# A decoder layer on one core: the written lists of steps of all engines laid out anew

## The reference

```python
def attn(x):                      # RWKV time mixing
    xs = shift x by one token
    k = (x * tm_k + xs * (1 - tm_k)) @ Wk.T      # v and r in the same way
    r = sigmoid(r)
    wkv = recurrence over tokens of k, v         # _wkv, a scan in time
    return (r * layernorm(wkv)) @ Wo.T
def xattn(x, ctx):                # the same kind of recurrence, k = norm(x), v = ctx
def ffn(x):                       # (silu(x @ G.T * gs) * (x @ U.T * us)) @ D.T * ds, inner width 1408
x = x + attn(layernorm(x)); x = x + xattn(layernorm(x), ctx); x = x + ffn(layernorm(x))
```

## Time and profile before

| what | value |
|---|---|
| median of 3 runs | 600.77 us (599.24 to 601.04) |
| the profiled execution | 598.28 us |
| its span in the trace | 596.4 us |
| PE busy | 536.3 us, 90% |
| DVE busy | 457.1 us, 77% |
| ACT busy | 345.4 us, 58% |
| POOL busy | 53.4 us, 9% |

### The profile page before, as it was taken

How to read it: one execution, slowest core, us unless ns; L and a number is a source line. 1 busy time by engine, 2 the same in 40 slices (tenths; PEclk the granted TensorE clock), 3 DMA queues, 4 the chain that set the end, 5 groups by cost and what they waited for, 6 DMA issues and landing times.

```text
span 596.4 us, 8018 instructions
## 1 busy us (share of the span) xinstructions
PE 536.3 (90%) x2658; PEld 381.6 (64%) x2658; DVE 457.1 (77%) x742; ACT 345.4 (58%) x546; POOL 53.4 (9%) x155
## 2 busy tenths in 40 slices
PE   2998589677799999999889999999969999999995
PEld 2443444323398446885689446786768699989994
DVE  5999778996977489999857589999856499852433
ACT  4737783467868257676557447766644486634221
POOL 2000300101022003000103003000011100000000
PEclk9999699988989999999979999999979999999998
DMA  8999700012100000001060000001040010010001
GB/s 304 414 315 385 291 0 2 18 35 87 48 26 2 1 1 0 1 19 53 1 213 0 0 0 1 0 18 53 0 142 0 1 38 36 0 36 1 2 36 38
DMA packets 14261, 39.02 MB, mean 65 GB/s; under 512 B 1232, under 2 KB 1232, under 8 KB 14032
## 3 DMA queue, kind: packets, MB, share of 16 engines
q1 hardware_dynamic: 14224, 38.57, 18.0%
HBM read 34.37 MB, written 12.85 MB: 79 GB/s over the span
## 4 chain that ended last, share of the span: by engine, by line
issue 38%; PE 34%; DVE 15%; POOL 6%; ACT 5%; DMA 1%; DVEq 0%; POOLq 0%; SPq 0%; ACTq 0%
PE gu L722 13%; PE dacc L650 7%; PE bank L636 6%; PE bank L698 5%; PE bank L625 3%; POOL t_rstd L598 2%; DVE t_slot L954 2%; DVE t_st L1091 1%; ACT L745 1%; DVE t_slot L1099 1%; DVE t_otile L1149 1%; DVE t_slot L1046 1%; POOL t_veps L596 1%; ACT t_z L799 1%; DVE t_xf L1116 1%
## 5 line engine op out<-in xcount | busy, mean ns | idle before, releaser
L722 PE MATMUL gu<-t_z4h,t_gate 128*128 128x256 f32 x352 | 94.1, 299 | 7.9 <-DVE t_z4l L1123 7.5
L722 PE MATMUL gu<-t_z4l,t_gate 128*128 128x256 f32 x352 | 89.3, 286 | 0.0
L722 PE MATMUL gu<-t_z4l,t_up 128*128 128x256 f32 x352 | 89.3, 286 | 0.0
L722 PE MATMUL gu<-t_z4h,t_up 128*128 128x256 f32 x352 | 89.2, 285 | 0.0
L879 ACT ACTIVATE t_h<-gu,t_fsc 128x256 f32<-128x256 f32 x88 | 40.4, 472 | 67.3 <-PE gu L722 65.8
L722 PEld LDWEIGHTS gu<-t_z4h,t_gate 128*128 128x128 f32 x352 | 68.4, 194 | 12.7 <-issue 10.4
L650 PE MATMUL dacc<-t_down,t_hh 128*128 128x512 f32 x176 | 72.5, 412 | 1.8 <-DVE t_hl L973 1.8
L722 PEld LDWEIGHTS gu<-t_z4l,t_gate 128*128 128x128 f32 x352 | 68.3, 194 | 2.4 <-issue 1.7
L650 PE MATMUL dacc<-t_down,t_hl 128*128 128x512 f32 x176 | 69.0, 392 | 0.0
L1128 DVE SCALAR_TENSOR_TENSOR t_h<-gu,t_fsc,t_h 128x256 f32<-128x256 f32 x88 | 40.6, 476 | 36.0 <-ACT t_h L879 35.9
L722 PEld LDWEIGHTS gu<-t_z4h,t_up 128*128 128x128 f32 x352 | 68.1, 193 | 0.0
(11 more groups left out here) (129 smaller groups left out, 930.5 us busy)
## 6 DMA issues: line engine op xcount, KB each, us to landing
t_mixv<-in_x SPq DMA_DIRECT2D x8, 512.0 KB, 6.0
t_xres<-in_x SPq DMA_DIRECT2D x8, 512.0 KB, 5.5
t_ctxt<-in_ctx_t SPq DMA_DIRECT2D x16, 256.0 KB, 2.8
out<-t_otile SPq DMA_DIRECT2D x16, 256.0 KB, 2.2
gate_words<-in_gate_t SPq DMA_DIRECT2D x1, 2816.0 KB, 17.1
up_words<-in_up_t SPq DMA_DIRECT2D x1, 2816.0 KB, 24.3
t_gate<-gate_words SPq DMA_DIRECT2D x1, 2816.0 KB, 15.5
down_words<-in_down_t SPq DMA_DIRECT2D x1, 2816.0 KB, 23.1
```

The lines of the kernel that those rows point to most:

```text
L722: last = pe.matmul(gu[u % 2][:, side, :], as_read(w[:, k, i * P:(i + 1) * P], exact), as_read(part[:, k, hf * HALF:(hf + 1) * HALF], exact ...
```

## The change

Every list of steps is written in a new order. The set of steps of each engine is the same, and so are the instructions of each step; one wait is added (`tanh_done` ahead of each `rw` on DVE). On PE, in the start, the output projection `wo` of batch 0 stands right behind `turn1+`, ahead of all projections of batch 1, and `y` of batch 0 behind `v2+`. In a round, `k0` to `k3`, `v0`, `v1` of the next batch stand ahead of `wo`, and `r0`, `r1`, `r2` come ahead of `turn3`; in the last stages only neighbours are exchanged. On SP the large transfer `words2` stands ahead of the loads of batch 1, and in a round the loads of the next `x` come first.

```diff
     PE_FIRST = """
-        turn1 k0 k1 v0 v1 k2 k3 v2 v3 r0 r1 r2 r3 turn2 return2 turn1+ k0+ k1+ v0+ wo v1+ turn3 r0+ r1+
-        r2+ r3+ y k2+ k3+ v2+ v3+ turn4_0 flag
+        turn1 k0 k1 v0 v1 r0 k2 k3 v2 r1 r2 v3 r3 turn2 return2 turn1+ wo k0+ k1+ v0+ v1+ turn3 r0+ r1+
+        r2+ r3+ k2+ k3+ v2+ y v3+ flag turn4_0
         """.split()
     PE_BODY = """
-        up0 up1 turn4_1 up2 turn2 up3 up4 up5 return2 down0 up6 down1 turn1 up7 wo k0 k1 v0 k2 k3 down2
...
+        up0 turn4_1 up1 turn2 up2 up3 up4 return2 up5 down0 down1 up6 turn1 down2 down3 up7 k0 k1 v0 v1
+        k2 k3 up8 wo v2 v3 r0 r1 r2 up9 turn3 up10 down4 up11 down5 down6 up12 down7 up13 down8 down9
+        down10 up14 up15 r3 down11 down12 down13 up16 up17 up18 up19 down14 down15 up20 up21 down16 y
+        down17 down18 down19 down20 down21 turn4_0
         """.split()
     DVE_FIRST = """
...
-        mixr0+ mixr1+ mixr2+ mixr3+ nv0+ num0+ part0+ den1+ x1_0 x1_1 x1_2 x1_3 fin0+ norm4 nv1+ norm5
...
+        mixr3+ x1_0 x1_1 x1_2 x1_3 norm4 front0+ norm5 front1+ den0+ nv0+ num0+ part0+ nv1+ den1+ num1+
...
     SP_FIRST = """
-        words1 xload0+ xload1+ words2 ctx2 ctx3
+        words1 words2 xload0+ xload1+ ctx2 ctx3
         """.split()
     SP_BODY = """
-        ctx0 ctx1 rload0 rload1 xload0 xload1 ctx2 ctx3 out0 out1 out2 out3
+        xload0 xload1 ctx0 ctx1 rload0 rload1 out0 out1 ctx2 ctx3 out2 out3
         """.split()
...
                 elif kind(s) == "rw":
                     c = int(s[2:])
                     need(dve, lnt_done, b, c + 1)
+                    need(dve, tanh_done, b, c + 1)
```

More of the change, by code:

```diff
@@ L98, in decoder_layer @@
-        tanh1+ tanh2+ xfront3 xpart2 tanh3+ xpart3 weigh2 sq6 weigh3 front2+ front3+ weigh4 norm6 weigh5
-        part2+ z4_0_0 z4_0_1 part3+ flag
+        share_r1 share_r2 share_r3 front0 front1 part0 tanh0 part1 front2 front3 weigh0 part2 tanh1
+        tanh2 tanh3 part3 weigh1 weigh2 norm2 norm3 rw0 rw1 rw2 rw3 norm0+ norm1+ share_k0+ share_k1+
+        share_k2+ share_k3+ share_v0+ share_v1+ share_v2+ share_v3+ share_r0+ share_r1+ share_r2+
+        share_r3+ sq4 sq5 front0+ front1+ norm4 norm5 part0+ weigh3 part1+ xfront0 xfront1 weigh4 weigh5
@@ L100, in decoder_layer @@
+        xpart0 xpart1 xfront2 tanh0+ xfront3 tanh1+ xpart2 xpart3 tanh2+ tanh3+ front2+ front3+ sq6
+        norm6 part2+ z4_0_0 z4_0_1 part3+ flag
         """.split()
     ACT_BODY = """
[L103 to L106, removed]
@@ L107, in decoder_layer @@
-        silu15 high6 xfront0 high7 xfront1 silu16 silu17 xpart0 high8 xpart1 xfront2 xfront3 silu18
-        silu19 tanh0 tanh1 tanh2 tanh3 xpart2 high9 xpart3 silu20 silu21 high10 sq6 norm6 z4_0_0 z4_0_1
+        sq7 norm7 z4_1_0 z4_1_1 silu0 silu1 high0 silu2 norm2 norm3 silu3 high1 rw0 rw1 silu4 rw2 rw3
+        norm0 norm1 silu5 high2 share_k0 share_k1 share_k2 share_k3 share_v0 share_v1 share_v2 share_v3
+        silu6 silu7 high3 front0 front1 part0 share_r0 share_r1 share_r2 part1 front2 share_r3 silu8
@@ L130, in decoder_layer @@
[L130 to L133, removed]
+        stat1_0 stat1_1 norm0 norm1 mixk0 mixk1 mixk2 mixk3 mixv0 mixv1 mixv2 mixv3 mixr0 mixr1 front0
+        mixr2 mixr3 front1 nv0 nv1 den0 num0 part0 den1 num1 part1 fin0 front2 fin1 front3 nv2 den2 num2
@@ L134, in decoder_layer @@
+        front3+ nv2+ den2+ num2+ xf_0 xf_1 xf_2 xf_3 part2+ den3+ nv3+ flag norm6 num3+ part3+ fin2+
+        z4_0_0 z4_0_1 fin3+
         """.split()
     DVE_BODY = """
[L137 to L144, removed]
+        norm7 z4_1_0 z4_1_1 prod0 prod1 stat2_0 stat2_1 prod2 norm2 rest0 norm3 prod3 stat1_0 stat1_1
@@ new lines, in decoder_layer @@
+        rest1 prod4 norm0 norm1 prod5 rest2 mixk0 mixk1 mixk2 mixk3 mixv0 mixv1 mixv2 prod6 mixv3 rw0
+        rw1 rw2 rw3 prod7 front0 front1 den0 nv0 nv1 num0 part0 den1 num1 mixr0 mixr1 fin0 part1 front2
+        fin1 front3 x1_0 mixr2 x1_1 x1_2 rest3 mixr3 den2 x1_3 nv2 num2 nv3 part2 den3 num3 part3 fin2
+        norm4 fin3 prod8 norm5 prod9 xfront0 xfront1 xin0 xden0 xnum0 xpart0 prod10 xin1 prod11 rest4
+        xden1 xnum1 xpart1 prod12 rest5 prod13 xfin0 xfront2 rest6 out0 out1 prod14 xfin1 xfront3 xin2
@@ L145, in decoder_layer @@
+        xden2 xnum2 prod15 xin3 prod16 xpart2 prod17 xden3 rest7 xnum3 prod18 prod19 rest8 xpart3 xfin2
+        xfin3 rest9 prod20 prod21 xf_0 xf_1 rest10 out2 norm6 out3 xf_2 xf_3 z4_0_0 z4_0_1
         """.split()
     DVE_NEXT = """
-        norm7 prod0 z4_1_0 z4_1_1 prod1 prod2 stat2_0 stat2_1 prod3 rest0 norm2 norm3 rw0 rw1 rw2 rw3
-        prod4 x1_0 x1_1 prod5 norm4 x1_2 rest1 rest2 x1_3 norm5 prod6 prod7 xfront0 xfront1 xin0 xden0
-        xnum0 xin1 prod8 prod9 xpart0 xden1 xnum1 rest3 xpart1 prod10 prod11 xfin0 rest4 xfront2 rest5
@@ L151, in decoder_layer @@
-        xfin1 prod12 prod13 xfront3 out0 out1 xin2 prod14 prod15 xden2 rest6 xnum2 prod16 rest7 prod17
-        xpart2 xden3 prod18 xin3 xnum3 prod19 xpart3 xfin2 xfin3 rest8 xf_0 xf_1 rest9 prod20 prod21
+        norm7 z4_1_0 z4_1_1 prod0 prod1 stat2_0 stat2_1 prod2 norm2 norm3 prod3 rw0 rw1 rw2 rw3 x1_0
+        rest0 x1_1 prod4 prod5 rest1 x1_2 x1_3 norm4 norm5 prod6 xfront0 xfront1 xin0 xin1 xden0 prod7
+        rest2 xnum0 prod8 rest3 xpart0 prod9 xden1 xnum1 xpart1 prod10 prod11 rest4 xfin0 xfin1 xfront2
@@ L153, in decoder_layer @@
+        rest5 xfront3 prod12 prod13 xden2 xin2 rest6 xin3 prod14 out0 prod15 out1 xnum2 prod16 xpart2
+        prod17 xden3 xnum3 rest7 xpart3 prod18 prod19 xfin2 xfin3 rest8 xf_0 xf_1 rest9 prod20 prod21
         norm6 rest10 z4_0_0 z4_0_1 out2 out3 xf_2 xf_3
@@ L170, in decoder_layer @@
     POOL_NEXT = """
[L171 removed]
+        nb7 rn7 rn2 rn3 nb4 nb5 rn4 rn5 nb6 rn6
         """.split()
```

48 lines of the change are left out of this document (22 added, 26 removed).

## The result

The changed kernel takes 604.7 us (median of 10 runs, 602.48 to 651.22) against 600.39 of the kernel before in the same session (10 runs, 597.96 to 601.04): a ratio of 1.0072, with a 95% interval of 1.0059 to 1.0085. I had forecast 599.2. (The run of 651.22 had a mean granted clock of 0.82, against 0.94 to 0.95 in the others, and isn't in the ratio.) The profiled execution took 604.17 us, its span is 602.2, against 598.28 and 596.4.

A forecast was written before the change was run, and what follows sets the result against it. The prediction took VectorE to bound the start and PE the rounds. Its terms, +1.0 for the start, -1.0 for each of two rounds and -0.6 for the last stages, gave 600.8 - 1.6 = 599.2 us, range 595.4 to 603.2.

The forecast's parts named there:

- `words2` ahead of the loads: Start, SP: batch 1's loads land behind `t_down`, so its statistics start at 70.4, 2.6 us later.
- the rest of the start, `wo` first: Start: `wo` first delays `front0+` to 98.05 but leaves VectorE less work and fewer waits behind it; -1.6 us.
- rounds and last stages: Two rounds at -1.0 us each and the last stages at -0.6: -2.6 us together.
- The step that failed: VectorE: the added wait on `tanh_done` concerns work that ended some 10 us earlier, so it costs nothing.
- Its other half: Head of a round: `turn4_1` one `up` earlier costs nothing, as `xf_3` moves up 0.6 us; without cover 0.6.
- `wo` ahead of the projections: Start, PE: `wo` runs 79.65 to 94.6, losing 1.2 us to the low clock, bounds 0.4 and 2.1.
- my slower rival: Start: `front0+` is later still, as `turn1+` ends later or `wo` runs longer at low clock; 603.2 us, chance 0.22.
- my 1.0: Each round 1.0 us shorter, bounds -1.5 and +1.5.
- the waits of 0.70, 0.48 and 0.19: Rounds, PE: the waits ahead of `down10`, inside `y` and ahead of `down20` go, gross 1.4 us.
- the 0.4 that I kept back for `y`, `xin2` and `wo`: Rounds: 0.4 us of the gross 1.4 left for possible new waits of `y`, `xin2` and `wo`.
- the 2.06 and 2.49 stay: Rounds, PE: the waits of 2.06 us ahead of `turn4_0` and 2.49 ahead of `up0` remain.
- The last stages: Next stage: the 0.57 us wait ahead of `turn4_0` goes; last stage keeps PE full; -0.6 us, bounds -1.0 and 0.

The follow-up runs named there:

- padding: The change with eight one-column memsets added at the start of VectorE's list: 598.38 us, ratio 0.9962 to the kernel before.
- The mixture: Against the kernel before: new start lists but old order of the loads on SP, old rounds and last stages, eight memsets on VectorE: 600.68 us, ratio 0.9999.
- its partner's: The kernel before with eight one-column memsets at the start of VectorE's list and nothing else: 601.12 us, ratio 0.9997.
- the padded kernel with the old loads: The change with batch 1's loads again ahead of `words2` on SP in the start, and eight memsets on VectorE: 595.42 us, ratio 0.9906.
- the mixture with the old start: The change with all engines' start lists as before, new rounds and last stages, eight memsets on VectorE: 598.20 us, ratio 0.9951.
- before, four memsets: The kernel before with four one-column memsets added at the start of VectorE's list: 602.56 us, ratio 1.0025.
- the change, loads held back: The change, with SP holding each round's six loads until VectorE has written the last z4 of the batch before: 598.37 us, ratio 0.9959.
- the change without the first waits: The change without the added wait on `tanh_done` for the four `rw` of batch 0: 599.53 us, ratio 0.9997.

## Why the prediction was wrong, point by point

The ledger, each line a difference of medians (some pairs from two sessions, whose medians of the kernel before differ by 0.3 us at most). The lines are links of one chain of kernels, so that their sum comes near the whole by construction and is no check of its own:

| part | predicted | measured | between |
|---|---|---|---|
| `words2` ahead of the loads | +2.6 | +3.0 to +3.6 | three pairs |
| the rest of the start, `wo` first | -1.6 | -0.4 (within the scatter) | 600.68 and 601.12 |
| rounds and last stages | -2.6 | -5.3 and -5.6 | 595.42 and 600.68; 598.38 and 603.95 |
| the code's position: padding | 0 | +6.3 | 604.7 and 598.38 |
| of it, the four added waits alone | 0 | +5.2 | 604.7 and 599.53 |
| sum, with 6.3 for the position | -1.6 | +3.3 to +4.2 | the change: +4.3 |

**The step that failed: "The added wait on `tanh_done` concerns work that ended some 10 us earlier: nothing."** True of the wait and false of its instruction. Its four for batch 0 moved the loop by four instructions in VectorE's code, and the branch back to the head then needed a second fetch before `norm7`. Without them the change takes 599.53 us, nearly the 599.2 of the forecast, though by errors that cancel, as the ledger shows.

**Its other half: "`turn4_1` comes one `up` earlier ... I cost it at nothing; without that cover it would be 0.6."** I counted the cover against `xf_3` alone. A second fetch ahead of `norm7` costs the kernel before 2.0 us, with two `up`s in front of `turn4_1`, and the change 6.3 with one. The trace of the kernel before has a row of VectorE that idles 2.65 us at that place, which the prediction doesn't look at: the branch and the first fetch lie in it, and the loop's first instruction ran only 0.6 us ahead of `norm7`.

**The order of the loads** was right in kind and short in size. The first row of VectorE's statistics of batch 1 in the changed kernel, and SP's queue:

```profile
54.69 0.37 SPq L529 DMA_DIRECT2D t_down<-down_words  x1
55.10 5.06 SPq L494 DMA_DIRECT2D t_mixv<-in_x  x1
...
70.66 1.28 DVE L980 BATCH_NORM_STATS2 t_stats<-t_mixv 128x6 f32<-128x512 f32 x2 [3.33 <-DMA t_mixv<-in_x]
```

70.66 stands against 70.4 forecast and 67.83 before. The transfers land in the order of issue: `t_down` at 69.3, the halves at 70.6 and 71.9, where I had 69.0, 70.4 and 71.7. Loads that pass `t_down`, which the second half of the rule quoted from the Trainium skill ("DMA: Bandwidth & Descriptors", "Queues, rings and completion order") would have allowed, didn't show.

**`wo` ahead of the projections** is mis-sized by the clock. PE in the changed kernel, from the turn on:

```profile
77.25 1.97 PE L625 MATMUL bank<-t_ident,t_mixv 128*128 128x128 f32 x8 [0.89 <-DVE t_mixv L988]
79.94 16.13 PE L698 MATMUL bank<-t_wo,t_tanh_r 128*128 128x512 f32 x32 [0.72 <-ACT t_zt L810]
95.90 5.31 PE L636 MATMUL bank<-t_mixk,t_wk 128*128 128x512 f32 x12
...
79.94:96.07 16.13, 16.13 (x33) 7.11 (x34) 10.19 (x18) 9.58 (x18) 1.43 (x5) 0.87 0.00 0
```

`wo` took 16.13 us and not 13.75, at a mean granted clock of 0.87: 2.4 us lost, where I had bounds of 0.4 and 2.1 and took 1.2. The clock stayed at 1.2 GHz until 84.3, 4.3 us into `wo`. VectorE's scan behind `k0+` began at 99.54, 1.5 us later than forecast (98.05), and the first `up0`, forecast at 166.3, came at 167.71. VectorE's part was right: from `front0+` to the end of `z4_0_1` (167.56) it took 68 us, as summed. With the larger loss my -1.6 becomes -0.4. The mixture measured -0.4 too, but its runs and its partner's spread over 3 to 4 us, so the agreement to a tenth is luck. That VectorE's whole chain hangs on `k0+` was the mechanism of my slower rival; it made 1.5 us here, and the 101.5 from which that rival would decide was not reached.

**The rounds** gained more than the forecast. The first round became 1.5 us shorter against my 1.0: the waits of 0.70, 0.48 and 0.19 are gone in full, and the 0.4 that I kept back for `y`, `xin2` and `wo` wasn't needed. In the padded kernels a round is shorter by 2.1 to 2.9 us than with the old lists after the same start. Round two of the padded kernel with the old loads, and of its partner with the old lists:

```profile
301.69:435.99 134.30, 129.50 (x665) 94.27 (x665) 113.86 (x181) 87.76 (x139) 12.36 (x36) 0.98 0.09 32
```

```profile
302.43:439.33 136.90, 130.75 (x664) 94.42 (x665) 112.52 (x181) 83.59 (x135) 14.58 (x36) 0.97 0.09 31
```

Of the 2.6 us, 1.35 are waits and 1.25 PE's busy time. Some 0.5 of the latter is the clock at the head of the round, where PE's wait ahead of `up0` is 2.06 us and not 2.75: the granted clock was back at 2.4 GHz 3.3 us into the round and not 4.3. Where the rest lies isn't shown. I had said "the 2.06 and 2.49 stay". The first does; the second falls at this boundary and stays at the next (2.74). Of the half of the gain that the mixture with the old start lacks, its first round shows a part (136.2 us and not 135.1, with the wait of 1.73); its runs spread over 5.7 us, and the rest stays open.

**The last stages**: -0.6 forecast, -0.7 and +0.4 measured in the profile; the wait ahead of the last `turn4_0` is gone.

## What to carry to other kernels

Where the profile gives "issue" as the releaser, directly behind a branch, look at the instruction queue before looking at the work. In a kernel with a loop, an instruction added anywhere ahead of the loop moves all of its code, so a difference of 1% between two orders isn't a difference between the orders until both have been timed with a few instructions of padding. One amount isn't enough: in the kernel before four instructions cost 2.0 us and eight nothing. So count the "instruction" packets and look where they fall. And the work that PE needs first in a round is best not put on VectorE right behind its branch, nor 2.5 MB of loads beside it: in this kernel the loads put the second packet 5.2 us behind the first and not 2.5.

## What the runs showed of the hardware

- A loop round of VectorE ran without any fetch of code when eight instructions were added ahead of the loop (14 fetches in place of 19), and with five fetches when none or four were. So here more code ahead meant fewer fetches.
- Where no code was fetched, the loop's first instruction on VectorE started 0.35 us behind the branch. Where it was, it started 1.8 to 1.9 us behind the start of the first packet. In four kernels (the change and the second to fourth row) `norm7` waited for the second packet and started 1.8 to 1.9 us behind it:

| second round of | 1st packet | loop's first instruction | 2nd packet | input of `norm7` | `norm7` |
|---|---|---|---|---|---|
| the change, padded | none | 302.71 | none | 306.45 | 306.49 |
| before, four memsets | 304.17 | 306.02 | 308.49 | 306.56 | 310.25 |
| the change, old order of loads | 304.42 | 306.24 | 309.59 | 306.25 | 311.50 |
| the change, loads held back | 303.81 | 305.71 | 306.33 | 306.87 | 308.20 |
| the change without the first waits | 308.74 | 310.62 | 313.92 | 309.05 | 310.74 |

- The gap of VectorE ahead of `norm7` was 2.55 to 3.03 us where no code was fetched (and then POOL's), 4.42 with a second fetch and the DMA engines nearly idle, and 6.28, 8.03 and 8.63 with a second fetch beside 2.5 MB of loads.
- The change with the old order of the loads spread over 7.7 us without padding and 3.4 with it. That fetches make the spread isn't shown: the padded mixture with the old start spread over 5.7 us, and the change with the loads held back, which fetches, over 2.1.
